# Context first, W's rows laid out for 128-partition transfers, and a new start-up order in a fused grouped convolution and LoRA feed-forward kernel

## What is computed

```
y   = conv1d(x, weight, groups=4, 9 taps, pad 4) + (cond_128 @ c_weight.T)[:, :, None] + bias_c[None, :, None]
out = x + y @ W + b + y @ (gate-mixed A_b).T @ (gate-mixed B_b).T + y @ A_s.T @ B_s.T
```

## Time and profile before

| what | value |
|---|---|
| median of 3 runs | 512.62 us (512.35 to 513.14) |
| the profiled execution | 513.78 us |
| its span | 512.0 us |
| PE busy, share of the span | 491.4 us, 96% |
| DVE, ACT, POOL busy | 337.2, 166.6, 273.0 us |
| mean granted clock of PE, share of full | 0.996 |

### The profile page before, as it was taken

How to read it: one execution, slowest core, us unless ns; L and a number is a source line. 1 busy time by engine, 2 the same in 40 slices (tenths; PEclk the granted TensorE clock), 3 DMA queues, 4 the chain that set the end, 5 groups by cost and what they waited for, 6 DMA issues and landing times.

```text
span 512.0 us, 6820 instructions
## 1 busy us (share of the span) xinstructions
PE 491.4 (96%) x2400; PEld 405.3 (79%) x2400; DVE 337.2 (66%) x385; ACT 166.6 (33%) x208; POOL 273.0 (53%) x158
## 2 busy tenths in 40 slices
PE   3998989799999999999999999999999999999995
PEld 3876768688888888888888888888888888888884
DVE  3976588695957579375957579375957579373401
ACT  2556412342333224241334224241333224241000
POOL 1778964395565718392565718392565718392100
PEclk9999999899999999999999999999999999999999
DMA  8996688623573409442573409442573403241303
GB/s 207 311 228 229 128 236 208 180 93 83 134 170 96 123 10 215 114 117 68 136 174 89 123 10 212 116 117 68 134 171 97 121 16 87 71 120 65 95 29 82
DMA packets 19575, 65.05 MB, mean 127 GB/s; under 512 B 3274, under 2 KB 3914, under 8 KB 18922
## 3 DMA queue, kind: packets, MB, share of 16 engines
q1 hardware_dynamic: 17690, 63.46, 47.4%
q10 hardware_dynamic: 1872, 1.41, 1.1%
HBM read 45.59 MB, written 18.87 MB: 126 GB/s over the span
## 4 chain that ended last, share of the span: by engine, by line
PE 87%; DVE 5%; DMA 4%; issue 1%; ACT 1%; POOL 0%; ACTq 0%; DVEq 0%
PE main L937 62%; PE rank L950 5%; PE main L942 3%; DMA lb<-in_L_ffn_lora_B 3%; PE conv L891 3%; PE conv L892 3%; PE conv L893 3%; PE conv L867 2%; PE main L915 1%; DVE x_tr L622 1%; PE spare L893 1%; PE spare L892 1%; PE spare L891 1%; DMA cw_nat<-in_L_cond_c_weight 1%; DVE x_tr L661 1%
## 5 line engine op out<-in xcount | busy, mean ns | idle before, releaser
L937 PE MATMUL main<-w_hi,y_hi 128*128 128x512 f32 x512 | 159.9, 391 | 2.4 <-DVE res L772 2.4
L937 PE MATMUL main<-w_hi,y_lo 128*128 128x512 f32 x512 | 159.0, 389 | 0.0
L937 PE MATMUL main<-w_lo,y_hi 128*128 128x512 f32 x512 | 158.2, 390 | 0.0
L387 POOL TENSOR_TENSOR y_lo<-y_stage,y_hi 128x512 fp32r<-128x512 f32 x56 | 94.2, 1703 | 41.0 <-ACT y_hi L498 41.0
L937 PEld LDWEIGHTS main<-w_lo,y_hi 128*128 128x128 f32 x512 | 96.0, 188 | 20.8 <-POOL w_lo L392 0.3
L937 PEld LDWEIGHTS main<-w_hi,y_hi 128*128 128x128 f32 x512 | 94.8, 188 | 22.4 <-POOL y_lo L381 2.8
L937 PEld LDWEIGHTS main<-w_hi,y_lo 128*128 128x128 f32 x512 | 96.1, 188 | 20.3
L367 POOL TENSOR_TENSOR xd_lo<-xd,xd_hi 128x512 fp32r<-128x512 f32 x28 | 40.2, 1435 | 101.6 <-ACT xd_hi L509 101.6
L369 POOL TENSOR_TENSOR x_lo<-x_tr,x_hi 128x1024 fp32r<-128x1024 f32 x28 | 82.3, 2938 | 14.8 <-ACT x_hi L511 14.8
L511 ACT ACTIVATE x_hi<-x_tr 128x1024 fp32r<-128x1024 f32 x28 | 57.5, 2054 | 30.4 <-DVE x_tr L661 30.4
L498 ACT ACTIVATE y_hi<-y_stage 128x512 fp32r<-128x512 f32 x56 | 35.5, 634 | 96.4 <-DVE y_stage L679 96.4
(11 more groups left out here) (105 smaller groups left out, 497.8 us busy)
## 6 DMA issues: line engine op xcount, KB each, us to landing
res<-in_x SPq DMA_DIRECT2D x32, 512.0 KB
out<-res SPq DMA_DIRECT2D x31, 512.0 KB
x_in<-in_x SPq DMA_DIRECT2D x28, 512.0 KB, 11.4
w_raw<-in_L_ffn_kernel SPq DMA_DIRECT2D x16, 256.0 KB, 19.1
b_cur<-b_scratch SPq DMA_DIRECT2D x21, 128.0 KB, 3.0
la<-in_L_ffn_lora_A SPq DMA_DIRECT2D x4, 512.0 KB, 11.0
lb<-in_L_ffn_lora_B SPq DMA_DIRECT2D x1, 2048.0 KB, 14.4
b_scratch<-be_hi SPq DMA_DIRECT2D x4, 256.0 KB, 4.6
```

Of the source, the lines that this page charges most:

```text
L387: nc.gpsimd.tensor_tensor(y_parity(y_lo, h, t, e), y_staged(e), y_parity(y_hi, h, t, e).bitcast(F32), ALU.subtract).then_inc(ylo_done, 1)
L937: mm(main[t][:, n * 512:(n + 1) * 512], lhs, rhs[:, k, n * 512:(n + 1) * 512], start=k == 0 and first, stop=False)
```

## The change

It rearranges W on the host (outside the timed program) so that each of four 1 MB parts is 128 rows of 8 KB, and loads each with one DMA to all 128 partitions (4 DMAs in place of 16). The context matrices go first on SP; the second half of x (all four pieces, on SP) goes behind lora_A and the first part of W; all shared A and B go on SP. The context's bias is no longer four matmuls with a row of ones: one small matmul with a selection matrix (`sel`, made on POOL) spreads it over the partitions, ACT copies it to `cb_col`, and DVE adds it while it copies the context. The taps' transposes come first on PE. `cw_rep` is made on ACT, no longer on DVE. The rest is order, on all five queues; the convolution's product order swaps its last two products.

More of the change, by code:

```diff
@@ L106, in adaln_ffn @@
         y_add, y_stage = sb("y_add", [P, 2, 512]), sb("y_stage", [P, 2, 512])
-        (w_pad, cond_nat, cw_nat, cond_t, cw_rep, cbias, bias_rep, ones, gate_nat, gate_rep, diag) = early(
+        (w_pad, cond_nat, cw_nat, cond_t, cw_rep, cbias, cb_col, sel, gate_nat, gate_rep, diag) = early(
             ("w_pad", [C, CG, PAD + TAPS + PAD], F32), ("cond_nat", [NS, CD], F32), ("cw_nat", [C, CD], F32),
-            ("cond_t", [CD, NS], F32), ("cw_rep", [P, G, J, CG], F32), ("cbias", [1, C], F32),
-            ("bias_rep", [1, G, J, CG], F32), ("ones", [1, NS], F32), ("gate_nat", [NB, NL], F32),
+            ("cond_t", [CD, NS], F32), ("cw_rep", [P, G, J, CG], F32), ("cbias", [CG, G], F32), ("cb_col", [P, G], F32), ("sel", [CG, J, CG], F32),
+            ("gate_nat", [NB, NL], F32),
             ("gate_rep", [NB, NL, R8], F32), ("diag", [P, R8], F32))
@@ L221, in _ @@
         def _(sp):
-            sp.dma_start(cbias[:, :], cond_bias.rearrange("(a c) -> a c", a=1)).then_inc(cbias_in, 16)
+            sp.dma_start(cond_nat[:, :], cond).then_inc(cond_in, 16)
+            sp.dma_start(cw_nat[:, :], cond_w).then_inc(cond_in, 16)
+            load_first(sp, 0, (0, 1))
+            with nc.allow_non_contiguous_dma(reason="sixty-four words"):
+                sp.dma_start(cbias[:, :], cond_bias.rearrange("(g c) -> c g", g=G)).then_inc(cbias_in, 16)
             sp.dma_start(gate_nat[:, :], gate).then_inc(gate_in, 16)
-            load_first(sp, 0, (0, 1))
-            load_shared(sp, 0)
-            load_shared(sp, 1)
-            load_first(sp, 1, (0, 1))
+            for q in range(3):
+                load_shared(sp, q)
             for oh in range(2):
@@ L467, in _ @@
                                      ACT.Copy).then_inc(thi_done, 1)
-            nc.scalar.activation(t01_raw[:, :, :, :].rearrange("p g s c -> p s g c"),
-                                 main[0][:, 512:1024].rearrange("p (s g c) -> p s g c", s=J, g=G), ACT.Copy).then_inc(t01_copied, 1)
+            act.wait_ge(cond_tr, 1)
+            nc.scalar.activation(cond_t[:, :], rank[:, 0:NS], ACT.Copy).then_inc(cond_cp, 1)
+            nc.scalar.activation(cw_rep[:, :, :, :], rank[:, NS:NS + C].rearrange("p (g c) -> p g c", g=G)
+                                 .unsqueeze(2).broadcast_to([P, G, J, CG]), ACT.Copy).then_inc(cwrep_done, 1)
+            nc.scalar.activation(cb_col[:, :], rank[:, 128:128 + G], ACT.Copy).then_inc(cond_cp, 1)
             act.wait_ge(gate_in, 16)
@@ L479, in _ @@
             x_first_high(0)
+            act.wait_ge(tlo_done, 2)
+            nc.scalar.activation(t01_raw[:, :, :, :].rearrange("p g s c -> p s g c"),
+                                 main[0][:, 512:1024].rearrange("p (s g c) -> p s g c", s=J, g=G), ACT.Copy).then_inc(t01_copied, 1)
             act.wait_ge(as_in, 48)
@@ L688, in w_add @@
                 k, half = m // 2, slice((m % 2) * 512, (m % 2 + 1) * 512)
-                dve.wait_ge(kern_in[k // 2], 64)
+                dve.wait_ge(kern_in[k // 2], 16)
                 dve.wait_ge(w_mm, m + 1)
@@ L722, in _ @@
             a_turn(0)
+            dve.wait_ge(t01_copied, 1)
             nc.vector.tensor_tensor(t01_raw[:, :, :, :].rearrange("p g s c -> p s g c"),
@@ L742, in _ @@
             y_tile(0, 0, 3, FIRST, first=True)
[L743 to L746, removed]
+            for m in range(8, 12):
+                w_add(m)
             dve.wait_ge(t01_split, 2)
@@ L753, in _ @@
             b_turn(3)
+            w_add(14)
+            w_add(15)
             nc.vector.memset(x_in[:, :, 0:HALO], 0.0).then_inc(halo_zero, 1)
             nc.vector.memset(x_in[:, :, HALO + L:], 0.0).then_inc(halo_zero, 1)
-            for m in range(14, 16):
-                w_add(m)
             nc.vector.memset(ax_st[STACK:ROWS, :].bitcast(F32), 1.0).then_inc(ones_put, 1)
@@ L827, in _ @@
             pe.wait_ge(ident_ready, 2)
-            pe.wait_ge(cond_in, 32)
-            nc.tensor.transpose(rank[:, 0:NS], cond_nat[:, :], ident[0:NS, 0:NS])
-            nc.tensor.transpose(rank[:, NS:NS + C], cw_nat[:, :], ident[0:C, 0:C]).then_inc(cond_tr, 1)
             pe.wait_ge(z_done, 1)
@@ L837, in _ @@
                 last.then_inc(t_tr, 1)
-            pe.wait_ge(cond_cp, 1)
+            pe.wait_ge(cbias_in, 16)
+            pe.wait_ge(sel_done, 1)
+            mm(rank[:, 128:128 + G], sel[:, :, :].rearrange("a j c -> a (j c)"), cbias[:, :],
+               start=True, stop=True)
+            pe.wait_ge(cond_in, 32)
+            nc.tensor.transpose(rank[:, 0:NS], cond_nat[:, :], ident[0:NS, 0:NS])
+            nc.tensor.transpose(rank[:, NS:NS + C], cw_nat[:, :], ident[0:C, 0:C]).then_inc(cond_tr, 1)
+            pe.wait_ge(cond_cp, 2)
             pe.wait_ge(cwrep_done, 1)
-            pe.wait_ge(biasrep_done, 2)
             for g in range(G):
-                cols = rank[:, 256 + g * NS:256 + (g + 1) * NS]
-                mm(cols, cw_rep[:, g, :, :].rearrange("p j c -> p (j c)"), cond_t[:, :], start=True, stop=False)
-                last = mm(cols, bias_rep[:, g, :, :].rearrange("a j c -> a (j c)"), ones[:, :], start=False, stop=True)
+                last = mm(rank[:, 256 + g * NS:256 + (g + 1) * NS], cw_rep[:, g, :, :].rearrange("p j c -> p (j c)"),
+                          cond_t[:, :], start=True, stop=True)
             last.then_inc(ctx_mm, 1)
```

12 lines of the change are left out of this document (2 added, 10 removed).

## The result

The changed kernel takes 507.64 us (median of 4 runs, 506.91 to 507.86), the kernel before 512.88 (4 runs); the ratio is 0.9894, 95% interval 0.9868 to 0.992. The profiled execution took 507.86 with a span of 506.0, against 513.78 and 512.0: 6.0 us less span. That is faster, as forecast. It is 2.4 us above the forecast value of 505.2 and outside the forecast's own range (503.8 to 507.0); it lies in the wide range (502.6 to 509.0) that takes in the rivals.

A forecast was written before the change was run, and what follows sets the result against it. PE, busy 491.4 of 512.0 us, bounds the kernel; only the first 110 us are in play. Gains of 2.8 + 3.0 + 1.6 = 7.4 off the 512.62 median give 505.2 us; own range 503.8 to 507.0, with rivals 502.6 to 509.0.

The forecast's parts named there:

- the rival that gives the front nothing: Start-up: x or context late, POOL's row starts at 41.0 as before; only 3.0 + 1.6 won, 508.0 us; chance 0.17.
- The low-rank stall: PE's wait for the low-rank operand of unit(0, 1): ax_high(1) going first on ACT removes 3.0 us, 0.5 to spare.
- The clock behind it: Matmuls after the low-rank operand's wait in unit(0, 1): the clock no longer falls, 1.6 us won.
- The front: Start-up up to the start of unit(0, 1): that start moves from 74.69 to 71.9, 2.8 us gained.
- 12.6, before 15.04: Start of PE's first convolution, in us: forecast at 12.6, where the kernel before had 15.04.
- again take 5.0: The 24 convolution matmuls of two tiles take 5.0 us, if the clock opens about 4 us behind the first convolution.
- POOL's row: POOL's gapless work from 38.9 us, 28.0 long, ending at 66.8; ax_steps(0)'s last subtraction ends with it.
- lora_B: Its transfer lands at about 37, before PE asks at 42.9; PE's 1.6 us wait for it goes.
- B: b_first, behind load_x(1) issued at 53.3 instead of 55.30, lands 2 us sooner, about 67.5, for PE's lowrank.
- The second: lowrank's wait returns if x_hi, L661 or ACT's xd_hi is late: up to 3.0 + 1.6 lost, 509.8; chance 0.08.
- The third: DVE's subtraction slips between two POOL operations, ending about 65.6; 1.2 to 2.0 better, 503.5 us; chance 0.08.
- The fourth: Slower: PE's clock opens late in the two first convolutions, 12.6 to 17.6 us, after new pauses; chance 0.05.

The follow-up runs named there:

- run 1: Kernel before with one edit: ACT runs ax_high(1) and a_high(1) ahead of x_high(2, 0, 1). 508.39 us, ratio 0.991.
- run 2: Changed kernel with one swap taken back: ACT again runs x_high(2, 0, 1) ahead of ax_high(1) and a_high(1). 512.91 us, ratio 0.9992.
- run 4: Kernel before with only W's new layout and its four transfers, all orders as before. 512.47 us, ratio 0.9997.
- run 5: Changed kernel with the DMA of the context's bias issued right behind the two context matrices, ahead of x. 507.73 us.
- run 8: Changed kernel with the sum read by DVE's last subtraction of ax_steps kept in PSUM, not SBUF. 506.50 us, ratio 0.987.
- run 7: Changed kernel with POOL's order of before from w_low(3) on. 508.53 us, ratio 0.992.
- run 9: Changed kernel plus PSUM sum, w_add(2), w_add(3) before a_turn(3), finish(0, 0) before y_tile(0, 1, 3), next x's last two pieces behind b_first. 508.79 us, ratio 0.9922.

## Why the prediction was right, and where its sizes were off

The direction, the bound and the last two terms held; the first term did not, and with it the gain was 5.2 us by the medians, not 7.4. That the time lies in the range owes something to luck: the range was wide enough only because it took in the rival that gives the front nothing.

- *The low-rank stall*, forecast 3.0: 3.2 (from the start of `unit(0, 1)`, `lowrank` 20.05 us later before, 16.9 now). The margin of 0.5 was there: the operand at 89.78, its use at 90.34. Runs 1 and 2 show that this swap alone carries it.
- *The clock behind it*, forecast 1.6: 1.5 between these two traces. The two L942 took 1.22 us at the granted clock of 0.50, the two L945 0.63 at 1.00, and five of the matmuls behind them lost 0.15 to 0.2 each. It is not a fixed price: in runs 2 and 4 the clock stayed down for 6.8 us in place of 3.4, and the stretch from this `lowrank` to the next took 14.5 and 14.3 us, before 13.0, in the changed kernel 11.5.
- *The front*, forecast 2.8: **1.2. This is the term that was mis-sized.** It failed in two steps. First, "12.6, before 15.04": it was 13.88. The context's bias was there at 9.6, not 7.8, and x's first half at 9.3, not 7.5; I took 229 GB/s for x from 2 to 3 us on, but the DMA engines moved 62 GB/s from 2 to 3 us and 179 from 3 to 4, and full rate only behind that; the taps and the second context matrix landed at 3.7 and 4.1. (That their small pieces are the reason is not shown.) Run 5 shows that the bias alone would not have given it. The context's matmuls took 1.9, not 2.5, which gave 0.6 back. Second, "again take 5.0" for the two tiles: they took 5.4, since full speed came at 19.6 us as before (19.4), and not 4 us behind the first convolution. This second step is in part chance of the execution: in run 2, the same program up to there, the two tiles took 4.5, `unit(0, 1)` started at 72.70, and the front's gain would read 2.0. With the rest of the way to tile 2 (0.3 forecast and 0.6 lost) a lead of 2.0 became 0.2. POOL's row then started at 40.85, not 38.9. A sign that the forecast named against itself stood in the trace, PE waiting for `cbias`, and three that it named for itself were missed: the first convolution at 12 to 13, `mix_a` at 17.6, and, just, more than 350 GB/s while W arrives (346). x's second half landed at 25.4, not 23.6 (DVE waited 0.4 for it), and lora_B at 40.3, not 37, still ahead of PE (44.9).
- *POOL's row*, forecast 28.0 us long and decisive for `ax_steps(0)`: 27.2, and decisive; runs 4 and 8 show it from both sides. Against the row of before (41.01 to 69.34) it starts 0.2 sooner and ends 1.3 sooner, and that is the front's whole gain. Run 7 puts some 1.1 of it on POOL's new order, a saving that I never counted as one; so the start's lead of 1.2 us was worth little.
- *lora_B*: the wait went, as forecast, and its 1.6 us were not won for themselves (run 4).
- *B*: `lowrank(0)` waited 0.7 for it, and had it at 69.4, not 67.5: `load_x(1)` was issued at 55.4 and not at 53.3, since `b_turn(2)` came later. It cost nothing, because `finish` came later still.

Of the rivals: the first (front gives nothing, 508.0) was nearer to the median than the forecast, and its mechanism is nearly what happened: the context's chain came late and POOL's row started at 40.85, where it had said 41.0. Only the length of the row differed, 27.2 in place of 28.0, with which the front gave 1.2 and not nothing. The second came true only in run 9, by its mechanism: `lowrank`'s operand late against a `finish` that came sooner. The third did not occur: DVE did not slip in, its subtraction ended 0.3 us behind POOL's row here and in run 4; run 8 shows that it would have been worth 1.1 to 1.3. The fourth came true in kind but hardly in size: full speed opened at 19.6, later than the 17.6 at which its stretch ended, and cost 0.4 us in the two tiles. Its ground, the pauses ahead of the convolutions, is not shown: run 2 has the same pauses and opened 3.2 us behind its first convolution, see below. The median's own change, 5.2, is smaller than the 6.0 between the two profiled spans; the spread of the kernel before (512.35 to 515.99 in four runs) covers that.

## What to carry to other kernels

Where several engines feed one consumer, a lead on one of them is worth only what the slowest chain to the next meeting point moves too: here two true gains (run 4, where W's layout removed lora_B's wait, and PE's earlier start in run 9) came out as nothing or as a loss, and one swap of two instruction groups on a lightly loaded engine gave about 5 us. Look for a small operation whose duration is many times that of its like (4.06 against 0.42 us) and ask what it waits on; here one operand moved to PSUM brought it from 2.04 to 0.41 us (run 8), without any reorder. Where the clock fell behind a stall, PE paid for the stall more than once: 3.0 us of idle time and 1.5 more at the clock of 0.50.

## What the runs showed of the hardware

**A small DVE operation with two SBUF inputs waited until POOL paused, through several of POOL's operations.** The 32x256 subtraction took 4.06 us before (three of POOL's), 5.71 in run 4 and 2.04 in the changed kernel, and in each it ended 0.28 us behind POOL's row. It took 0.42 with POOL idle, and 0.41 beside a working POOL with one operand in PSUM (run 8). This is shown for that subtraction only, not for every such operation. In the same trace of the changed kernel two larger ones with both inputs in SBUF, 1.06 and 1.12 us long without POOL ahead of them (79.87 and 80.97), did get their turn while POOL worked from 96.26 to 102.59 without a gap, and POOL's operations became longer too (L397 took 1.72 us here, 0.86 in the start-up's row):

```profile
96.46 2.05 DVE L656 TENSOR_TENSOR xd<-x_tr 128x512 f32<-128x512 f32 x1
98.54 2.10 DVE L658 TENSOR_TENSOR x_tr<-x_tr 128x512 f32<-128x512 f32 x1
```

```profile
96.26 3.41 POOL L387 TENSOR_TENSOR y_lo<-y_stage,y_hi 128x512 fp32r<-128x512 f32 x2 [0.89 <-ACT y_hi L501]
99.63 1.72 POOL L397 TENSOR_TENSOR a_cur<-a_eff,a_cur 128x256 fp32r<-128x256 f32 x1
```

These two lost 1.0 us each and ended while POOL worked; the subtraction of before waited through three of POOL's operations. What sets the two cases apart is open. A wait behind a single operation also stands in the low-rank chain: L658 at 84.44 took 3.72 us, with one `x_low` on POOL until 87.18, and that chain has a margin of only 0.5 us.

**When PE first gets its full clock is not set by the program alone.** The changed kernel and run 2 have the same program until ACT's swap, behind 84 us, and both started the first convolution at 13.88. In run 2 the second tile's matmuls already shorten, and `mix_a(0)` starts at 18.34, not 19.30:

```profile
16.61 0.85 PE L870 MATMUL conv<-x_hi,t_hi 128*128 128x256 f32 x4
17.30 0.64 PE L870 MATMUL conv<-x_hi,t_lo 128*128 128x256 f32 x4
17.77 0.64 PE L870 MATMUL conv<-x_lo,t_hi 128*128 128x256 f32 x4
18.34 3.83 PE L918 MATMUL main<-la,gmix 128*32 128x128 f32 x64
```

The trace's record of full clock begins there at 17.1 us, at 19.6 in the changed kernel, at 21.0 in run 1. Counted from the first convolution that is 3.2 us (run 2) to 6.1 us (run 5) over the twelve traces, where the prediction took 4 as given. The two first tiles took 4.5 to 5.4 us by it: up to 1 us of PE's work by chance, as much as several edits above are worth.

**Nor is the clock's fall behind a stall.** Behind the stall of 2.9 to 3.0 us for the low-rank operand it fell to 0.50 in all three traces that have the stall, from 94.4 to 97.9 us before, but from 92.2 to 99.0 in run 2 and from 93.5 to 100.3 in run 4. Behind the 2.4 us stall for `finish` it fell in one of four traces (run 1, not before, run 4 or run 7), and behind 1.8 us in run 9; behind the 1.5 us of the changed kernel it did not. Much of the spread of the kernel before goes with it: of its 52 executions beside the runs above, the 13 with a mean granted clock of 0.992 or less took 513.45 to 515.81 us, the 10 with 0.999 or more 510.3 to 512.63. It is why the edits under 2 us had to be read at stations.
